# A layer of attention and product-key experts: the last tile's product moved from GpSimd to VectorE, and two TensorE steps moved within their queue

## What is computed

```
xn   = rmsnorm(x) * norm_w
q    = (xn @ w_q.T) split into 8 heads and 2 sides
s1,i1 = top 8 of 32 similarities of side 1;  s2,i2 = the same of side 2
all_sc = s1[:,None] + s2[None,:];  all_idx = i1[:,None]*32 + i2[None,:]
fs, pk = top 8 of all_sc;  fi = all_idx[pk]
hidden = gelu(xn . expert_down[fi]) * relu(fs)
out    = layernorm(x + sum(hidden * expert_up[fi]))
```

## Time and profile before

| | us |
|---|---|
| median of 3 runs | 1596.99 (1593.52 to 1597.36) |
| the profiled execution's own time | 1597.08 |
| its span, first to last instruction | 1595.2 |
| mean granted TensorE clock | 0.897 of full speed |
| VectorE busy | 1370.8 (86%) |
| TensorE matmuls busy | 1352.8 (85%) |
| ScalarE busy | 910.9 (57%) |
| GpSimd busy | 663.8 (42%) |

### The profile page before, as it was taken

One profiled execution on the slowest core, in us unless ns is written; L12 is line 12 of the kernel. 1 busy time (PEld: TensorE's weight loads), 2 busy tenths in 40 slices (PEclk: granted clock), 3 DMA queues, 4 the chain that ended last, 5 costly groups with the idle time before them and its releaser, 6 DMA issues.

```text
span 1595.2 us, 55196 instructions
## 1 busy us (share of the span) xinstructions
PE 1352.8 (85%) x21008; PEld 975.3 (61%) x21008; DVE 1370.8 (86%) x6598; ACT 910.9 (57%) x1486; POOL 663.8 (42%) x1024
## 2 busy tenths in 40 slices
PE   5676879899898989989898989989898988987577
PEld 4343457576566757666666747666675756665557
DVE  5337799989999989989999998989999998798985
ACT  3656757565666667566666657666666756442110
POOL 3307172552708163462708264461717254050410
PEclk7787989999999989999898989989898989988667
DMA  3000000000000000000000000000000000000000
GB/s 87 7 8 8 8 9 9 15 3 9 16 9 16 9 15 9 16 2 9 16 9 16 9 15 9 10 8 9 16 9 16 3 15 3 2 16 1 9 2 17
DMA packets 30004, 18.80 MB, mean 12 GB/s; under 512 B 1840, under 2 KB 29232, under 8 KB 29744
## 3 DMA queue, kind: packets, MB, share of 16 engines
q1 hardware_dynamic: 29744, 15.23, 3.3%
HBM read 11.04 MB, written 4.19 MB: 10 GB/s over the span
## 4 chain that ended last, share of the span: by engine, by line
PE 40%; DVE 37%; issue 8%; ACT 7%; POOL 6%; DVEq 0%; ACTq 0%; POOLq 0%
DVE onehot L1278 10%; PE G L934 7%; PE F L879 7%; PE OV L823 7%; DVE topi L1224 6%; PE G L923 5%; DVE psel L1240 4%; DVE topv L1218 3%; ACT prob L644 3%; DVE whot L1303 3%; PE S L809 3%; DVE fsel L1235 2%; DVE hid L1316 2%; PE S L748 2%; POOL qk_u L455 1%
## 5 line engine op out<-in xcount | busy, mean ns | idle before, releaser
L644 ACT ACTIVATE prob<-S 128x512 f32<-128x512 f32 x640 | 371.0, 595 | 148.6 <-PE S L811 142.0
L923 PE MATMUL G<-whot,onehot 128*128 128x16 bf16 x12288 | 383.3, 171 | 30.5 <-DVE hid L1316 19.2
L923 PEld LDWEIGHTS G<-whot,onehot 128*128 128x128 bf16 x12288 | 364.5, 97 | 64.5 <-issue 16.5
L1278 DVE TENSOR_TENSOR onehot<-lo_no,elo 128x1024 bf16<-128x1024 uint16 x512 | 385.7, 802 | 0.0
L823 PE MATMUL OV<-prob,vp 128*9 128x512 f32 (+3 forms) x2048 | 183.7, 508 | 68.3 <-ACT prob L644 62.0
L508 POOL TENSOR_TENSOR gat<-gat,cande 128x1280 f16<-128x1280 f16 x64 | 178.5, 2789 | 76.6 <-DVE gat L1246 76.6
L811 PE MATMUL S<-causal,ident_b 128*128 128x128 bf16 x1024 | 201.4, 229 | 0.0
L809 PE MATMUL S<-qT,kT_even 128*128 128x512 bf16 (+3 forms) x512 | 147.1, 316 | 55.0 <-ACT prob L644 46.9
L517 POOL COPY y<-y_new 128x512 f32<-128x512 f32 x16 | 9.8, 610 | 433.9 <-DVE r L1186 378.0
L573 ACT ACTIVATE hid<-F 128x512 f32<-128x512 f32 x128 | 76.5, 597 | 185.1 <-PE F L879 185.1
L823 PEld LDWEIGHTS OV<-prob,vp 128*9 128x9 f32 x2048 | 55.2, 100 | 197.1 <-issue 106.2
(11 more groups left out here) (144 smaller groups left out, 2515.8 us busy)
## 6 DMA issues: line engine op xcount, KB each, us to landing
xa<-in_L_attn_x SPq DMA_DIRECT2D x16, 256.0 KB, 2.8
xr<-in_L_attn_x SPq DMA_DIRECT2D x16, 256.0 KB, 2.8
out<-r SPq DMA_DIRECT2D x15, 256.0 KB, 2.3
onehot<-in_L_ffn_expert_down SPq DMA_DIRECT2D x1, 512.0 KB, 5.4
up<-in_L_ffn_expert_up SPq DMA_DIRECT2D x1, 512.0 KB, 7.2
onehot<-in_L_ffn_keys SPq DMA_DIRECT2D x1, 256.0 KB, 4.5
out<-r SPq DMA_DIRECT2D x2, 128.0 KB, 1.8
onehot<-in_L_attn_w_qkv SPq DMA_DIRECT2D x1, 192.0 KB, 3.1
```

The source lines that it names most:

```text
L644: act.activation(dst, src, ACT.Exp, scale=SCALE).then_inc(exp_done.sem, 1)
L923: last = nc.tensor.matmul(bank[:, 16 * i:16 * i + 16], onehot[:, row, :], whot[:, t, w_part, :], start=(w_part == 0), stop=(w_part == 2))
L1278: return dve.tensor_tensor(onehot[:, row:row + 8, :].rearrange("p t (c i) -> p t c i", i=2), lo, e, ALU.is_equal)
```

## The change

The product of tile 3, and only this, is made by VectorE right after its comparison, under a semaphore of its own, and GpSimd's product of tile 3 goes. On TensorE, in every step, the numbers and the selections' transposes stand directly behind the scores, ahead of the transposes of queries and keys and of the weights.

```diff
-        gat_done = signal("gat_done", NT)
+        gat_done = signal("gat_done", NT - 1)
+        last_gat_done = signal("last_gat_done", 1)
...
                     candidates(late, 3)
                     gather(late, 2)
-                    gather(late, 3)
...
-                pe.wait_ge(gat_done.sem, gat_done.value(b, t + 1))
+                if t < NT - 1:
+                    pe.wait_ge(gat_done.sem, gat_done.value(b, t + 1))
+                else:
+                    pe.wait_ge(last_gat_done.sem, last_gat_done.value(b, 1))
...
+                    if late is not None and step in NUMBER_STEPS:
+                        turn_numbers(late, NUMBER_STEPS.index(step))
+                    if late is not None and step == SELECTION_STEP:
+                        transpose_selection(late)
                     if nxt is not None and step in QK_STEPS:
                         transpose_stack(nxt, QK_STEPS.index(step), b)
                     if older is not None and step in WEIGHT_STEPS:
...
                         project_similarities(late, SIMS_STEPS.index(step))
-                    if late is not None and step in NUMBER_STEPS:
-                        turn_numbers(late, NUMBER_STEPS.index(step))
-                    if late is not None and step == SELECTION_STEP:
-                        transpose_selection(late)
...
+            def last_gather(b):
+
+                dve.wait_ge(hotc_done.sem, hotc_done.value(b, NT))
+                t = (NT - 1) % 2
+                dve.tensor_tensor(gat[:, t], gat[:, t], cande[:, t].rearrange("p h c -> p c h").unsqueeze(3)
+                                  .to_broadcast([P, NCAND, H, TOPK]), ALU.mult)\
+                    .then_inc(last_gat_done.sem, 1)
...
                 if late is not None:
                     top_pairs(late, 3)
+                    last_gather(late)
                 if b is not None:
                     normalise_o(b, 2)
```

## The result

The changed kernel takes 1640.3 us (median of 4 runs, 1633.76 to 1643.29) beside 1597.15 for the kernel before on the same chip: a ratio of 1.0274, 95% interval 1.0243 to 1.0305. Slower by some 43 us, well outside the range that was given, and slower where a little faster was forecast. The profiled execution took 1641.46 us, its span is 1639.7.

The account below looks back on a forecast made before the run. TensorE and VectorE were taken to end a full pass almost together, the chain then running through TensorE and ScalarE's copies. From 1597.08 us, +2.6 - 3.2 - 3.4 = -4.0 gave 1593.1 us, range 1585 to 1600.

Parts of the forecast that it names:

- The change part by part: The prediction's costing of moved product, moved numbers and selections, step 35 and three other passes, against 1597.08 us.
- the sum's -4.0: Whole kernel: +2.6 us for full passes, -3.2 and -3.4 for the last two, giving 1593.1 us.
- The product: Tile 3's product on VectorE: 1.7 us, first one-hot 0.68 instead of 2.83; a full pass gains a few tenths at most.
- Step 35: TensorE's numbers and selections ahead of q's transposes: decode over 2 us earlier, scores 37 waiting about 0.9 us for k's copy.
- Rival C: Scores 37's new wait lowers TensorE's granted clock: 2.1 us per pass, 27 us in all, about 1620; chance 0.11.
- A: The sum itself: mean +0.2 us per full pass, earlier ends, 1593.1 us, bounds 1587 to 1599; chance 0.68.
- +2.6 over 13: Full passes with weights, transposes and selections: scores 37 later by a mean +0.2 us each, bounds 0 to +5.
- The ends: Last pass with attention and the pass after: earlier decodes give -3.2 us and -3.4 us.
- B: ScalarE's copies don't hold scores 37, so freed waits are kept: some 10 us plus 6.6, about 1581; chance 0.13.
- D: Nothing changes: the two last passes wait instead for chunk 6, which TensorE completes after the numbers; 1597, chance 0.08.

Follow-up runs that it names:

- e2: Kernel before with only the second semaphore added, TensorE's loop three register instructions longer, no product or order moved: 1641.74 us, ratio 1.0312.
- e7: Changed kernel with the first instruction of TensorE's loop placed at slot 0 of a 256-instruction fetch block: 1592.44 us, ratio 0.9992.
- e8: Changed kernel with the first instruction of TensorE's loop placed at slot 128 of a fetch block: 1637.39 us, ratio 1.0267.
- e9: Kernel before, no instruction of its loop changed, with TensorE's loop placed at slot 128 of a fetch block: 1643.32 us, ratio 1.0303.
- e1: Changed kernel with both semaphores counted in fours, so TensorE's loop is as long as in the kernel before: 1596.8 us, ratio 1.0024.
- e3: Kernel before with only tile 3's product moved to VectorE, TensorE's old order, semaphores counted in fours: 1585.8 us, ratio 0.9945.
- e5: Changed kernel with semaphores in fours and the new order only in passes without a next q and k: 1581.56 us, ratio 0.9928.
- e6: Changed kernel with semaphores in fours and the transposes of q and k ahead of numbers and selections, then weights: 1582.08 us, ratio 0.9932.
- e10: As e6, with the first instruction of TensorE's loop placed at slot 0 of a fetch block: 1581.96 us, ratio 0.9919.

## Why the prediction was wrong

The step that failed is one that isn't there. The part "The change part by part" takes up the product and the moved instructions, but not the first lines of the diff, the second semaphore; the sum so has no term for what the edit adds to TensorE's own program. e2 shows that those lines alone cost as much (1641.74 us beside 1593.86 on its chip), e7, e8 and e9 that they cost it by the place of the loop. Per turn it is the wait at L823 (3.17 us instead of 0.27) and an attention that follows it at the lower clock (3.84 us instead of 2.34): 4.4 us in the pass shown, and 4.0 on average between e1's full pass and the changed kernel's. The trace of before had the sign of it: a wait for "issue" of 0.2 to 0.3 us at each turn, and one of 3.8 where the loop is left and TensorE goes on to other code. It wasn't read as a price that the loop could come to pay at every turn.

Without that term the rest can be held against e1: 2.9 us above the kernel before on its chip, "same" by the 0.3% used there, but at the far end of the range, and on the other side of the kernel before than the sum's -4.0.

*The product*: taken as 1.7 us, it took 1.49. This was the place where an estimate by the Trainium skill (Vector Engine (DVE) Microarchitecture Reference, 5.1 Performance modes) was about 1.5 us: the trace agrees, where the middle of two rows was 0.21 off. The prediction said that VectorE's gain could give a full pass a few tenths and no more, and its sum had nothing for it; e3 shows 0.26 us per pass, and e5, the same loop without the lower clock of e3's long passes, 0.94, though on another chip.

*Step 35*: scores 37 were predicted 5.51 us after scores 35 with a wait of about 0.9; measured 5.53 and 0.84. The decode was to come 2 us earlier; against scores 35 it came at 2.09 instead of 4.42.

*Rival C*, which lowers the clock behind that wait, had its mechanism right and its condition wrong. It was to decide only near a wait of 2.3 us, at 2.1 us per pass, as an alternative to A; e1 shows it behind 0.84 us in nine passes of eleven, at 0.67 on average in that stretch and more further on, beside A's +0.2, which the two other passes show. With all this, and with the product's gain in it, e1's full pass is 0.88 us longer than that of the kernel before: +9.6 us over 11 passes, where the prediction had +2.6 over 13.

*The ends*: -3.2 and -3.4 were worked out. From tile 3's comparison to the decode the last pass with attention takes 5.77 us in the changed kernel, the pass after it 5.74. VectorE's timeline there, beside the earlier trace rows, and then the two comparisons in the kernel before:

```profile
1484.49 0.83 DVE L1249 TENSOR_TENSOR gat<-psel,cand_no 128x1280 f16<-128x1280 uint16 x1
...
1490.26 0.68 DVE L1271 CAST hot_hi<-F 128x512 uint16<-128x512 f32 x1
...
1568.15 0.83 DVE L1249 TENSOR_TENSOR gat<-psel,cand_no 128x1280 f16<-128x1280 uint16 x1
...
1573.89 0.69 DVE L1271 CAST hot_hi<-F 128x512 uint16<-128x512 f32 x1 [0.38 <-PE F L902]
```

```profile
1433.12 0.83 DVE L1246 TENSOR_TENSOR gat<-psel,cand_no 128x1280 f16<-128x1280 uint16 x1
...
1520.63 0.82 DVE L1246 TENSOR_TENSOR gat<-psel,cand_no 128x1280 f16<-128x1280 uint16 x1
```

Before it was 9.54 and 9.44 us (decodes in the earlier trace rows): -3.8 and -3.7, so both steps were right, and a little small. The part behind the last copy shrank by 12.8, not 6.6; 5.9 us of that lie ahead of tile 3's comparison in the last pass with attention. e3 has 1.5 of those 5.9 by the product alone and e1 3.2. The 2.7 between e1 and the changed kernel go with the place of the loop again: the wait where the loop is left, 3.8 us before and 3.2 in e1, isn't there in the changed kernel, nor in e2 and e9, which have 2.3 and 4.0 of the 5.9 with no product and no order moved. This part of the gain is the loop's, and no term of the prediction.

*Rivals B and D*: B is out for the change as made, since the copies do hold scores 37; e6 shows what B meant, with another order. D is out, since the two ends did come earlier by what A had for them.

## What to carry to other kernels

When a change touches a long loop, count what it adds to each engine's own program, register arithmetic for waits included, and look at the first instruction of each turn: a wait there for "issue", with a packet on the instruction queue inside it, is the loop's place and nothing that the change meant. Test it by placing the loop before anything is concluded about the change. And put nothing that has time ahead of a chain that runs through another engine's copies (transposes, copies, scores): here the numbers cost 0.97 us per pass more ahead of the transposes than behind them, most of it by where the lower clock fell.

## What the runs showed that was not expected

The place of a loop in its blocks is worth 2.8 to 3.1% of this kernel: 1592.44 against 1637.39 us for one and the same body (e7, e8), and 1594.35 against 1643.32 for the kernel before (e9). The loop has a hint for its closing branch at the head of each turn, and still pays. In all these runs but those at slot 0 it pays in one of two ways: either at its eleven turns, or once where it is left (2.8 to 3.8 us); at slot 0 (e7, e10) it pays neither. Which slots pay beyond the two that were tried, and whether it is the place of the head or of the closing branch, wasn't tried.

A wait of 0.84 us was followed by a lower granted clock 1 to 2 us later, but not each time: with the same wait at 625.73 the clock stayed at 1.00. Where the lower clock falls decides what it costs: e6's passes differ by 1.6 us with it, behind the same wait of 0.80 us. Why it falls in one pass and not in the next, the runs don't show.

One kernel's executions differ by more than 0.3% on one chip: e1's ten runs lie between 1592.41 and 1601.98. Part of it lies in the first passes: the third copy of x stands at 101.70 us in e1's profiled execution and at 106.63 in the changed kernel's, though nothing of the change has run by then. Why was not looked into.
